# A sixteen-layer program: another schedule for the selective scan of its third sublayer, and slot-list routing for its last expert mixtures

## The reference, cut to what matters

```python
xz = einsum('bld,ed->ble', x, W_in);  u, z = split(xz, 2)
u_c = silu(causal_conv4(u, conv_w) + conv_b)
dt_r, Bm, Cm = split(einsum('bld,ed->ble', u_c, W_x), [8, 24])
dt = softplus(einsum('blr,dr->bld', dt_r, W_dt) + b_dt);  A = -exp(A_log)
def step(h, (dt_t, u_t, B_t, C_t)):            # h: [b, 256, 16]
    h = exp(dt_t[..., None] * A) * h + (dt_t * u_t)[..., None] * B_t[:, None, :]
    return h, einsum('bds,bs->bd', h, C_t)
y = (scan(step) + u_c * D) * silu(z);  out = einsum('bld,ed->ble', y, W_out)
```

```python
vals, idx = top_k(softmax(x @ Wg), 2);  w = vals / (vals.sum(-1) + 1e-9)
# first choices are ranked before second ones; a token past rank 256 of its expert is dropped
for e in range(8):
    ye = gelu(x @ W1[e] + b1[e]) @ W2[e] + b2[e]        # 128 -> 512 -> 128
    out += combine[:, e][:, None] * ye
```

## Time and profile before

| | |
|---|---|
| median of the runs shown | 4003.49 us |
| the profiled execution | 3992.1 us |
| its span in the trace | 3990.2 us |
| mean granted TensorE clock | 0.851 of full |
| busy: PE, DVE, ACT, POOL | 75%, 52%, 35%, 22% |
| sublayer 3 after its layernorm (699.4 to 1115.1) | 415.7 us |
| sublayer 14 after its layernorm (3417.2 to 3554.8) | 137.6 us |
| sublayer 16 after its layernorm (3847.0 to 3985.0) | 138.0 us |

### The profile page before, as it was taken

How to read it: one execution, slowest core, us unless ns; L and a number is a source line. 1 busy time by engine, 2 the same in 40 slices (tenths; PEclk the granted TensorE clock), 3 DMA queues, 4 the chain that set the end, 5 groups by cost and what they waited for, 6 DMA issues and landing times. The chain is left out here.

```text
span 3990.2 us, 57442 instructions
## 1 busy us (share of the span) xinstructions
PE 2983.1 (75%) x22506; PEld 1587.4 (40%) x22506; DVE 2068.2 (52%) x3648; ACT 1387.8 (35%) x2626; POOL 858.4 (22%) x623
## 2 busy tenths in 40 slices
PE   6666788565677699898688889886967578459954
PEld 3553266121266344344222234322234345445534
DVE  5211353696953688303888760275744535327630
ACT  4202433333333266523677752211012112124631
POOL 0000035493925210003543100000000002340023
PEclk9667779786889799999899999887988789778977
DMA  2021011000012311000311000000000001123201
GB/s 98 14 81 41 0 34 51 0 0 0 0 29 61 99 33 32 2 0 12 63 28 28 1 1 0 10 0 0 0 0 0 0 0 43 46 61 61 39 17 58
DMA packets 76696, 104.74 MB, mean 26 GB/s; under 512 B 13335, under 2 KB 50167, under 8 KB 75171
## 3 DMA queue, kind: packets, MB, share of 16 engines
q1 hardware_dynamic: 67363, 82.72, 8.8%
q0 software_dynamic: 9088, 18.63, 1.6%
HBM read 73.26 MB, written 27.82 MB: 25 GB/s over the span
## 5 line engine op out<-in xcount | busy, mean ns | idle before, releaser
L1629 DVE TENSOR_REDUCE at_mp<-PS 128x1 f32<-128x384 f32 (+3 forms) x640 | 313.6, 538 | 115.1 <-PE PS L1479 98.8
L1579 ACT ACTIVATE at_pt<-PS 128x384 f32<-128x384 f32 (+3 forms) x704 | 288.3, 456 | 212.2 <-PE PS L1491 176.6
L1476 PE MATMUL PS<-at_kx,at_qx 72*128 72x384 bf16 (+5 forms) x640 | 219.2, 347 | 66.4 <-DMA at_kx<-L_attn_a_parts 26.8
L1489 PE MATMUL PS<-at_qx,at_kx 105*128 105x512 bf16 (+5 forms) x704 | 214.1, 314 | 7.8 <-ACT at_pt L1579 5.9
L3908 DVE CUSTOM_DVE_ANT_0 PS<-PS,ls_pt 128x1024 f32<-128x1024 f32 x128 | 153.7, 1239 | 17.0 <-ACT ls_pt L3761 14.8
L3761 ACT ACTIVATE ls_pt<-PS,ls_far 128x512 f32<-128x512 f32 x256 | 155.3, 684 | 20.4 <-PE PS L3582 15.7
L2164 POOL TENSOR_TENSOR mb_bu<-mb_du,lnA 128x1024 f32<-128x1024 f32 x32 | 130.7, 4104 | 123.8 <-ACT lnA L2151 123.8
L2122 PE MATMUL PS<-mb_bcp,mb_sel 96*128 96x512 bf16 x128 | 45.9, 449 | 145.9 <-DVE mb_hc L2180 100.2
L2128 PE MATMUL PS<-mb_hc,ident 128*128 128x512 f32 x256 | 145.9, 724 | 0.7 <-DVE mb_hc L2180 0.5
L2164 POOL TENSOR_TENSOR mb_u<-mb_du,lnA 128x1024 f32<-128x1024 f32 x32 | 138.6, 4350 | 0.0
L1491 PE MATMUL PS<-at_above,identb 128*128 128x128 bf16 x704 | 133.7, 222 | 0.0
(11 more groups left out here) (814 smaller groups left out, 7106.0 us busy)
## 6 DMA issues: line engine op xcount, KB each, us to landing
dl_arena<-in_fir_bank SPq DMA_DIRECT2D x32, 256.0 KB, 3.1
ffn_place<-in_ffn_L SPq DMA_DIRECT2D x4, 1152.0 KB, 17.1
at_qx<-L_attn_a_parts SPq DMA_DIRECT2D x24, 192.0 KB
at_kx<-L_attn_a_parts SPq DMA_DIRECT2D x72, 64.0 KB
at_qx<-L_attn_b_parts SPq DMA_DIRECT2D x24, 192.0 KB
at_kx<-L_attn_b_parts SPq DMA_DIRECT2D x72, 64.0 KB
mx_s<-y_rows SPq DMA_DIRECT2D x16, 256.0 KB, 4.9
ffn_place<-in_ffn_L SPq DMA_DIRECT2D x4, 1024.0 KB, 8.2
```

What stands on the lines that cost most here:

```text
L1476: mm = nc.tensor.matmul(PS[:, n % 3, 0:e - c], QX[0:RAW, u % 3, g, blk(i, P)], KX[0:RAW, u % 3, g, c:e], start=True, stop=True)
L1489: mm = nc.tensor.matmul(PS[:, 3 + n % 3, 0:e - c], KX[0:FULL, u % 3, g, blk(j, P)], QX[0:FULL, u % 3, g, c:e], start=True, stop=True)
L1579: nc.scalar.activation(PT[:, y % SLOTS, g, 0:e - c], PS[:, 3 + n % 3, 0:e - c], ACT.Exp, scale=SCALE).then_inc(exp_done, 1)
L1629: nc.vector.tensor_reduce(best, sc, AX.X, ALU.max).then_inc(s_maxed, 1)
```

## The change

The kernel after differs in three ways.

1. **`l0b`, front.** The loop over batches is gone. Both batches' four blocks run through one stage: ACT now also applies the last tap of the convolution, softplus goes block by block, and one matmul makes dt's inputs, B and C together in fp32 (40 rows, `XD`). SP writes B (16 x 2048) to DRAM.
2. **`l0b`, scan.** One stage of 32 units u (batch s, state n) and 64 steps. SP reads a row of B back onto all partitions, 512 KB a unit, into a ring of four buffers; POOL multiplies into a ring of three; ACT writes the decays to two PSUM banks, one slot, so it waits for each scan; C is spread by a fp32 matmul of 40 rows; the scan's input 0 lies in PSUM. PE's three bf16 parts and the ACT copy of B go.
3. **`l3_ffn`.** The list form of `l0_ffn`, with two tiles an expert.

```diff
 def l3_ffn(k):
             def _(sp):
+                for b in range(NBLK):
+                    sp.wait_ge(rows_copied, b + 1)
+                    sp.dma_start(x_rows[blk(b), :]..., XT[:, TB * b:TB * b + TB, :]).then_inc(rows_stored, 16)
                 if fresh:
-                    sp.dma_start(slot_x[0:SLOTS, :]..., XS...).then_inc(cleared, 16)
-                sp.wait_ge(scattered, out_base + 16 * PAIRS)
-                for e in range(E):
-                    sp.dma_start(XS[:, e, :, :], slot_x[blk(e, CAP), :]...).then_inc(loaded[e // 2], 16)
-                for e in range(E):
-                    sp.wait_ge(y_taken, e + 1)
-                    sp.dma_start(slot_y[blk(e, CAP), :]..., Y[:, e, :, :]).then_inc(y_stored, 16)
+                    for q in range(2):
+                        sp.dma_start(y_rows[blk(q, NTOK), :]..., YG[:, q, :, :]).then_inc(cleared, 16)
+                sp.wait_ge(filled, fill_base + 16 * TILES)
+                for b in range(NBLK):
+                    for q in range(2):
+                        sp.dma_start(YG[:, q, TB * b:TB * b + TB, :], y_rows[...]...).then_inc(back[b], 16)
             def _(pool):
...
+                pool.wait_ge(rows_stored, 16 * NBLK)
+                pool.wait_ge(placed, 1)
+                fetch(0)
+                fetch(1)
+                fetch(2)
+                if fresh:
+                    pool.wait_ge(cleared, 32)
+                for e in range(E):
+                    if e + 3 < E:
+                        fetch(e + 3)
+                    fill(e)                     # waits y_taken >= e + 1
             def _(pe):
+                for q in range(2):
+                    for t in range(NTILE):
+                        pe.wait_ge(in_place, NTILE * q + t + 1)
+                        mm = nc.tensor.matmul(whose, INPLACE[:, q, t, :], PAYLOAD[:, q, t, :, :], ...)
+                mm.then_inc(found, 1)
             def place(q):                        # DVE
+                    for t in range(NTILE):
+                        nc.vector.tensor_scalar(INPLACE[:, q, t, :], PLACES[:, :], LOW[:, q, t:t + 1], None, ALU.is_equal).then_inc(in_place, 1)
...
 def l0b(k):
+        with stage(nc, "spread_0", ...):
+            def _(sp):
+                for u in range(UNITS):
+                    s, n = u // NS, u % NS
+                    if u >= 4:
+                        sp.wait_ge(bu_done, 2 * (u - 3))
+                    sp.dma_start(BS[u % 4], b_rows[n:n + 1, s * SEQ:(s + 1) * SEQ].to_broadcast([P, SEQ])).then_inc(spread[u % 4], 16)
+            def _(pool):
+                        pool.tensor_tensor(BU[:, m % 3, :], DU[:, u // NS, h, :], BS[u % 4], ALU.mult).then_inc(bu_done, 1)
+            def _(pe):
+                lines(0)                         # C of a unit: 2 fp32 matmuls
+                for u in range(UNITS):
+                    add(u, 0)                    # 2 fp32 matmuls with the identity
+                    if u + 1 < UNITS:
+                        pe.wait_ge(hc_done, 2 * u + 2)
+                        lines(u + 1)
+                    add(u, 1)
+            def _(act):
+                        if m:
+                            act.wait_ge(scanned, m)
+                        nc.scalar.activation(wide(6), DT[:, s, h, :], ACT.Exp, scale=A[:, h, n:n + 1]).then_inc(a_done, 1)
+                        if m == 2 * NS:
+                            for g in range(2):
+                                act.wait_ge(y_added, 2 * NS - 1 + g)
+                                nc.scalar.activation(YS[:, g, :], wide(2 * g), ACT.Identity).then_inc(y_kept, 1)
+            def _(dve):
+                        nc.vector.tensor_tensor_scan(HS, wide(6), BU[:, m % 3, :], 0.0, ALU.mult, ALU.add).then_inc(scanned, 1)
...
```

More of the change, by code:

```diff
@@ L446, in _ @@
+                sp.wait_ge(filled, fill_base + 16 * TILES)
+                for b in range(NBLK):
+                    for q in range(2):
+                        sp.dma_start(YG[:, q, TB * b:TB * b + TB, :], y_rows[q * NTOK + b * BLK:q * NTOK + (b + 1) * BLK, :].rearrange("(t p) d -> p t d", p=P)).then_inc(back[b], 16)
             @block.gpsimd
             def _(pool):
[L448 to L455 removed]
@@ L456, in _, with fetch @@
[L456 to L461, removed]
+                def fetch(e):
+                    for j in range(ST):
+                        at = ST * e + j
+                        pool.indirect_dma_start(out=XS[:, e, j, :], out_offset=None, in_=x_rows[:, :], in_offset=bass.IndirectOffsetOnAxis(ap=FROM[:, at:at + 1], axis=0)).then_inc(fetched[e], 16)
@@ L590, in _ @@
-                for t in range(NTILE):
-                    for q in range(2):
-                        m = nc.vector.tensor_scalar(DG[:, q, t, :], k.ident[:, :], GATE[:, q, t:t + 1], None, ALU.mult)
-                m.then_inc(diag_made, 1)
+                dve.wait_ge(found, 1)
+                own(nc.vector.tensor_copy(EMPTY[:, :], PS[:, 0, TILES:2 * TILES]))
+                own(nc.vector.scalar_tensor_tensor(out=WHOSE[:, :], in0=EMPTY[:, :], scalar=float(P), in1=PS[:, 0, 0:TILES], op0=ALU.mult, op1=ALU.add))
@@ L2007, in layer_constants @@
+        wide = lambda a: PS[:, a:a + 2, :].rearrange("p a b -> p (a b)")
         def layer_constants(pool, own):
-            own(pool.memset(U[:, :, 0:3], 0.0))
-            own(pool.memset(SELR[:, :, :], 0.0))
-            for part in range(3):
-                own(pool.affine_select(out=SELR[:, :, :], in_=SELR[:, :, :], compare_op=ALU.not_equal, fill=1.0, base=-32 * part, pattern=[[-1, 2 * NS], [0, P]], channel_multiplier=1))
+            own(pool.memset(SELC[:, :, :], 0.0))
+            own(pool.affine_select(out=SELC[:, :, :], in_=SELC[:, :, :], compare_op=ALU.not_equal, fill=1.0, base=-(R + NS), pattern=[[-1, NS], [0, P]], channel_multiplier=1))
+            for s in range(BATCH):
+                own(pool.memset(U[:, s, :, 0:3], 0.0))
@@ new lines, in _ @@
+                nc.scalar.activation(k.warm[:, 0:1], k.eps_col[:, 0:1], ACT.Silu)
+                take(0)
+                for b in range(1, NBLK):
+                    take(b)
+                    curve(b - 1)
+                curve(NBLK - 1)
+                nc.scalar.activation(k.warm[:, 0:1], k.eps_col[:, 0:1], ACT.Ln)
+                nc.scalar.activation(A[:, :, :], W[pre + "A_log"], ACT.Exp).then_inc(own_a, 1)
+                keep(0)
+                for b in range(NBLK):
+                    if b + 1 < NBLK:
+                        keep(b + 1)
+                    soften(b)
@@ new lines, in _, with convolve @@
+                own = Link(dve, own_d)
+                def convolve(b):
+                    s, at = place(b)
+                    for h in range(2):
+                        dve.wait_ge(tapped, 2 * b + h + 1)
+                        if b % 2:
+                            dve.wait_ge(u_kept, 2 * (b - 1) + h + 1)
+                        for j in range(3):
+                            ins = nc.vector.scalar_tensor_tensor(out=UC[:, s, h, at], in0=U[:, s, h, j + at.start:j + at.stop], scalar=W[pre + "conv_w"][:, h, j:j + 1], in1=UC[:, s, h, at], op0=ALU.mult, op1=ALU.add)
+                            if j < 2:
```

472 lines of the change are left out of this document (251 added, 221 removed).

## The result

The changed kernel takes 3820.2 us (median of 4, 3816.6 to 3823.5) against 4003.2 (3993.9 to 4005.4). The ratio is 0.9547, 95% interval 0.9528 to 0.9566: 183 us less, forecast 3814 and 3770 to 3865. A second series, beside some of the experiments, gave 3814.6 us and 0.9547 again (0.9529 to 0.9564).

The account below looks back on a forecast made before the run. DVE and POOL taking turns bound the scan, a chain of latencies the mixtures. Gains of 93.7 (sublayer 3) and 90 (two mixtures), 184 us, took the profiled 3992.1 to 3808, moved halfway to the median: 3814, range 3770 to 3865.

Parts of the forecast that it names:

- The lock: Scan stage: DVE's scan and POOL's multiplication take turns; with decays in PSUM this ends, step 3.68 us instead of 4.33.
- Rival A: Scan stage: one SBUF operand still makes scan and multiplication take turns; 42 us given back, 3856; chance 0.08.
- ACT's decays: Scan stage: with one slot, each decay takes 1.32 us against 1.39 available; cost taken as 0, at most 4 us.
- PE covered by 0.6: Scan stage: PE's spreads of C over the partitions take 1.8 us at full clock, the next product comes 2.46 later.
- rival B: Scan stage: PE at half clock binds, 97 us, 3911; only the spreads of C late, 38 us, 3852; chance 0.10.
- DMA hidden: Scan stage: four buffers hide B's 512 KB a unit of 7.36 us; only the first landing, 4.2 us, shows.
- Rival C: Scan stage: B's DMAs at 17.1 us each, one after the other, make the kernel slower, 4121; chance 0.02.
- Start and change of batch: Scan stage: 7.0 us until the first multiplication ends; ACT's two copies of y hold one decay up by 2.2.
- Front 58, tail 17: Sublayer 3 around the scan stage: front bound by ACT with ten table loads, 58 us; gating and matmuls after, 17 us.
- The mixture: Sublayers 14 and 16: POOL's DMA issues bind, end at 89.6 us against 137.6; gain taken as 45 each, 90 together.
- Rival D: Mixtures: POOL waits for each result before writing it, so the list form brings nothing; 20 less each, 3854; chance 0.08.
- own range: Whole kernel: 3785 to 3843 us, from the bounds of front, ACT and mixtures and the 11 between profile and median; chance 0.72.

Follow-up runs that it names:

- the grouped run: The changed kernel with all eight Exp and then all eight Ln in the front of the scan sublayer, instead of alternating by block: 3823.2 us, ratio 0.9556.

## Why the prediction was right, and where it was off

- **The lock (scan 2.29 beside POOL's 2.33, step 3.68).** Right: 64 scans of 2.291, POOL 2.355, step 3.67. The Trainium skill, "SBUF — State Buffer", Who interferes with whom, says that two SBUF inputs on DVE exclude a GpSimd instruction that reads SBUF. The trace and the decays' return to SBUF agree with it, 3.17 against 2.29. Rival A is out. The 42 us that A was to give back are less than the 51 found.
- **ACT's decays, covered by 0.07.** Right, and easier than thought: 1.118 us to PSUM, against the 1.15 of the earlier trace rows. No step waits for one.
- **PE covered by 0.6, at full clock.** Half wrong. At full clock the cover is there, 0.42 for 0.6: the lines end at 859.75, the product starts at 860.17; but the clock was 0.84, not over 0.9, and ten late lines cost 6.4 us. This is a small part of rival B, which I had priced at all or 38 us. The run without the lines gives 6.5 back.
- **DMA hidden.** Right, with a wide margin: 3.7 us to land, of 4.2 thought, and twice the bytes cost nothing behind the first. Rival C is out.
- **Start and change of batch.** 6.2 us for 7.0, and 4.0 for 2.2. The term of the copies was mis-sized: I counted their own length, but the second one first waits for PE's last sum (4.80 idle on ACT), and the decay is queued behind it. With PE's start the extras were put at 4.5, and they were 4.0 + 6.4: 251.4 for 247, the other 1.4 coming back in the start and in steps of 3.67.
- **Front 58, tail 17.** 57.7 and 14.7. The first was right for a reason that is only half right, and in part by luck. I called it bound by ACT, loads included. Busy ACT is 47.1 of 57.7, and with 9.3 less of it the front was 1.2 shorter: the way through PE's products and DVE's sums is about as long. And the same front takes 54.8 in four other executions. The Trainium skill, "ScalarE: Activation LUTs", Table sets: the hidden batching unit, names a set with both Exp and Ln; the trace doesn't show it in use, with seven loads of 1.28 us between the blocks' Exp and Ln. What such a set would bring in this order wasn't tried; the grouped run shows that 9 us less on ACT need not shorten the front.
- **The mixture.** First fetch 21.5 us in (22.8, where the terms given add up to 22.3), first result 37.6 (36.2), last issue 75.7 (74), end 91.3 (92.6, since 3 were taken off the gain). PE waits at the fifth expert as said, and at the seventh too. Of the 7 us of waits that I took as given (POOL's four after its first write add up to 8.5), the order of POOL's queue was the cause, and the other order takes 9 to 13 us away. Rival D is out. That the list form brings the gain is shown by its own run; how the gain divides within it is read from the timeline alone.
- **The sum.** 184 forecast, 185.2 by stretches, 183 by the medians. In sublayer 3 the scan took 4.4 more than forecast and tail and front 2.7 less, so a part of the closeness is luck. The profile-based 3808 was missed by 8.6 because 9.7 us of untouched stretches differed; going halfway to the median was a guard against that, and that it nearly sufficed is luck too. The own range of 3785 to 3843 doesn't follow from the bounds named for it: around 3814 they give 3792 to 3836, which holds the result as well.

## What to carry to other kernels

When two engines' busy times look like a shared bound, look whether one instruction is longer beside the other engine's than alone; then moving one operand to PSUM can be worth more than moving work (51 us here, in a stage that the whole rewrite shortened by 35). Price a wait by what is queued on the same engine, not by the length of the waiting instruction. A queue that both fetches and writes back is best given all the fetches that have buffers first.

## What the runs showed of the hardware that was not expected

- With two SBUF inputs the scan waits for the rest of POOL's instruction, inside its own recorded length (3.20 us, up to 4.35), and POOL's record stays at 2.36 where it was first. Where POOL came second, its record is the long one: 4.36 from 780.37, behind a scan from 779.65.
- An activation of 1024 columns into PSUM took 1.118 us, into SBUF 1.148.
- One 4 KB row of DRAM read 128 times (512 KB) was usable 3.7 us after its issue, and 131 GB/s of it beside DVE and POOL lengthened neither.
- PE was granted 0.84 in a stage in which it is busy 85% of the time, and 0.95 when a third of its work was left out (busy 56%).
